# Rotary embedding from even-column and odd-column tiles of four heads, in place of a second up product with swapped columns

## The reference, cut to what matters

```python
q = (c_q @ w_up_q.T).reshape(b, s, 16, 64).transpose(0, 2, 1, 3)     # k likewise, from c_kv
e, o = (x[..., 0::2], x[..., 1::2])                                  # _apply_rope, q and k
rot = jnp.stack([e * cos - o * sin, e * sin + o * cos], axis=-1).reshape(x.shape)
scores = jnp.einsum('bhqd,bhkd->bhqk', q, k) * scale                 # softmax over these
out = jnp.einsum('bhqk,bhkd->bhqd', attn, v)
```

## Time and profile before

| | us |
|---|---|
| median of 3 runs | 1811.61 (1811.47 to 1812.64) |
| the profiled execution | 1810.62 |
| its span | 1808.7 |
| TensorE busy | 1649.7 (91%) |
| VectorE busy | 1577.7 (87%) |
| ScalarE busy | 1309.1 (72%) |
| GpSimd busy | 1306.5 (72%) |

### The profile page before, as it was taken

The page is one execution under the profiler, slowest core; times in us unless marked ns, Lnnn a source line. Parts: engine busy times, 40 slices in busy tenths (PEclk is TensorE's granted clock), DMA queues, the critical chain, the costliest instruction groups (busy, mean ns, idle before and its releaser), DMA issues. The chain is left out here.

```text
span 1808.7 us, 50674 instructions
## 1 busy us (share of the span) xinstructions
PE 1649.7 (91%) x20016; PEld 1027.2 (57%) x20016; DVE 1577.7 (87%) x3235; ACT 1309.1 (72%) x1876; POOL 1306.5 (72%) x926
## 2 busy tenths in 40 slices
PE   3888756999999999999999999999999999968888
PEld 2444431666666666666666666666666666644555
DVE  6999886999999998999999998999999998848885
ACT  4555462888888888888888888888888888855554
POOL 2343523888888888888888888888888888643444
PEclk9999976999999999999999999999999999988999
DMA  5000003111111112211111112211111112000000
GB/s 170 1 2 1 1 1 70 37 37 37 37 37 37 37 41 52 53 37 37 37 37 37 37 40 54 52 37 37 37 37 37 37 39 52 20 1 1 13 13 25
DMA packets 46665, 63.49 MB, mean 35 GB/s; under 512 B 9312, under 2 KB 21600, under 8 KB 46176
## 3 DMA queue, kind: packets, MB, share of 16 engines
q1 hardware_dynamic: 43632, 59.41, 13.7%
q10 hardware_dynamic: 2800, 0.85, 0.2%
HBM read 7.67 MB, written 2.10 MB: 5 GB/s over the span
## 5 line engine op out<-in xcount | busy, mean ns | idle before, releaser
L1222 POOL TENSOR_TENSOR area<-area 128x1024 f16<-128x1024 f32 (+1 forms) x512 | 833.1, 1645 | 159.9 <-ACT area L1190 137.7
L1116 DVE TENSOR_REDUCE area<-ps 128x1 f32<-128x512 f32 x1024 | 668.8, 685 | 60.5 <-PE ps L996 52.4
L1188 ACT ACTIVATE area<-ps 128x1024 f16<-128x1024 f32 x512 | 524.6, 1025 | 233.8 <-PE ps L1023 233.0
L1042 PE MATMUL ps<-cv_all,area 128*128 128x64 f16 x4096 | 458.6, 195 | 0.0
L1040 PE MATMUL ps<-cv_all,area 128*128 128x65 f16 x4096 | 456.8, 193 | 1.5 <-POOL area L1222 1.5
L1044 PE MATMUL ps<-cv_all,area 128*128 128x65 f16 x4096 | 455.3, 192 | 0.0
L1042 PEld LDWEIGHTS ps<-cv_all,area 128*128 128x128 f16 x4096 | 381.3, 97 | 86.1
L1040 PEld LDWEIGHTS ps<-cv_all,area 128*128 128x128 f16 x4096 | 384.0, 97 | 51.6 <-POOL area L1222 1.4
L1022 PE MATMUL ps<-area 128*128 128x512 f16 x1024 | 390.0, 381 | 18.6 <-DVE area L1140 17.7
L996 PE MATMUL ps<-area 128*128 128x512 f16 x1024 | 394.8, 386 | 8.6 <-DMA area<-area 5.7
L1023 PE MATMUL ps<-area 128*128 128x512 f16 x1024 | 388.7, 380 | 0.0
(11 more groups left out here) (175 smaller groups left out, 2727.9 us busy)
## 6 DMA issues: line engine op xcount, KB each, us to landing
area<-area SPq DMA_DIRECT2D x384, 128.0 KB, 2.4
xg<-in_x SPq DMA_DIRECT2D x4, 512.0 KB, 7.5
area<-in_wup SPq DMA_DIRECT2D x1, 2048.0 KB, 10.5
out_x<-xg SPq DMA_DIRECT2D x3, 512.0 KB, 3.2
cs<-in_rope SPq DMA_DIRECT2D x1, 1024.0 KB, 11.5
area<-area SPq DMA_DIRECT2D x64, 2.0 KB
area<-in_wo ACTq DMA_DIRECT2D x1, 512.0 KB, 7.5
area<-in_wg SPq DMA_DIRECT2D x1, 512.0 KB, 8.4
```

What stands on the lines that cost most here:

```text
L1042: nc.tensor.matmul(o[:, 0:DH], p_hi[:, s % 4, c:c + P], latents[:, DH + 1:CV], start=False, stop=False, skip_group_check=True)
L1116: nc.vector.tensor_reduce(mx[:, hd, kh, qt:qt + 1], bank, AX.X, ALU.max).then_inc(s_mr, 1)
L1188: nc.scalar.activation(p_hi[:, s % 4, :], sc, ACT.Exp, scale=0.125).then_inc(s_e16, 1)
L1222: nc.gpsimd.tensor_tensor(p_lo[:, s % 4, c0:], src[:, (s // 2) % 2, :], p_hi[:, s % 4, c0:], ALU.subtract).then_inc(s_pp, 1)
```

## The change

Weight columns are split in even and odd ones (`up_columns`), 128 of each hold 32 pairs of four heads, and a chunk now serves four heads, which is two units (a group). An R item is the up product of the even or of the odd columns; each is multiplied by cosine and by sine (2 VectorE instructions an item), and GpSimd makes `even*cos - odd*sin` and `odd*cos + even*sin` (2 instructions a chunk). ScalarE casts both in one instruction of 1024 columns; GpSimd makes the low halves in two. A unit now runs 2 chunks: 4 R items in steps 6, 7, 14 and 15. A head's 64 rows now lie in `qk` as 32 even and 32 odd ones, which come from two tiles: `stack` copies 32 partitions at a time, 24 copies a unit. The buffers grow (`area` from 26 to 30 K words, r_hi and r_lo to three buffers of two halves). The plan of items is new, and so is the prologue: 14 R items (7 chunks), and the first scores are issued 6 items before its end. The transposition of the maxima uses the plain identity, and the factor 1/64 moves to the VectorE instruction behind it.

```diff
-            "aa aaa aT Tmrb rb Prbb rbb Pbbb bb rbbb rbb rccn rc ccc cc cc".split())}
+            "aa aaaa Tm Tbb Pb Pbbb rb rbb bb bbbb bcn ccc c ccc rc rc".split())}
...
-        before = [letters[c].pop(0) for c in "rrrrrrrrssssaaaaaassaaaaaassaaaambbbbbbbbbb"]
+        before = [letters[c].pop(0) for c in "rrrrrrrrrraaaaaarraaaaaarraaaambbbbbbbbbb"]
...
+        SUMS, CASTS, LOWS = {1: (6, 0), 3: (6, 1), 9: (7, 0), 11: (7, 1)}, {4: 6, 12: 7}, {5: (6, 0), 7: (6, 1), 13: (7, 0), 15: (7, 1)}
...
                     elif kind == "A":
                         if i == 0 and hd == 0:
-                            pe.wait_ge(s_sq, (w + 1) * 96)
-                            pe.wait_ge(s_sk, (w + 1) * 96)
+                            pe.wait_ge(s_sq[slot], (w // 2 + 1) * 192)
+                            pe.wait_ge(s_sk[slot], (w // 2 + 1) * 192)
...
-                        nc.vector.tensor_tensor((ra, rb)[sw][:, c % 2, :], bank, cs[:, sw, 512 * half_:512 * half_ + 512],
-                                                ALU.mult).then_inc(s_mr, 1)
+                        nc.vector.tensor_tensor(ra[:, c % 2, i, :], bank, cos, ALU.mult)
+                        nc.vector.tensor_tensor(rb[:, c % 2, 1 - i, :], bank, sin, ALU.mult).then_inc(s_mr, 1)
...
-                    nc.gpsimd.tensor_tensor(rc[:, c % 2, :], ra[:, c % 2, :], rb[:, c % 2, :], ALU.add).then_inc(s_rc, 1)
+                    nc.gpsimd.tensor_tensor(rc[:, c % 2, i, :], ra[:, c % 2, i, :], rb[:, c % 2, i, :],
+                                            (ALU.subtract, ALU.add)[i]).then_inc(s_rc, 1)
...
-                    nc.scalar.copy(r_hi[:, c, :], rc[:, c % 2, :]).then_inc(s_rh, 1)
+                    nc.scalar.copy(r_hi[:, b_, h_], rc[:, c % 2]).then_inc(s_rh, 1)
...
                 def stack(w, slot):
-                    for kind, done in ((0, s_sq), (2, s_sk)):
-                        for sm in (s_rh, s_rl):
-                            sp.wait_ge(sm, w * 4 + (kind + 2))
+                    for kind, done in ((0, s_sq), (1, s_sk)):
+                        sp.wait_ge(s_rh, 4 * group + 2 * kind + 2)
+                        sp.wait_ge(s_rl, 2 * (4 * group + 2 * kind + 2))
                         for hd in range(2):
-                            rows = slice(64 * hd, 64 * hd + 64)
-                            hi, lo = (t[rows, kind:kind + 2, :].rearrange("p c n -> p (c n)") for t in (r_hi, r_lo))
+                            head = 2 * (w % 2) + hd
+                            for i in range(2):
+                                hi, lo = (t[32 * head:32 * head + 32, b_, :, i, :] for t in (r_hi, r_lo))
...
-                                sp.dma_start(qk[name_][row:row + 64, slot, hd, :], src).then_inc(done, 16)
+                                    row += 32 * i
+                                    sp.dma_start(qk[name_][row:row + 32, slot, hd, :].rearrange("p (h n) -> p h n", h=2),
+                                                 src).then_inc(done[slot], 16)
```

More of the change, by code:

```diff
@@ L33 @@
 UNITS = B * PAIRS
+GROUPS = UNITS // 2
+HALF = H * DH // 2
 EPS = 1e-5
@@ L46, in rope_tables @@
     sin = np.concatenate([np.sin(freqs), np.sin(freqs)], -1)[:, ::2]
[L47 to L50, removed]
+    return np.stack([np.tile(cos.T[:DH // 2], (4, 1)), np.tile(sin.T[:DH // 2], (4, 1))], 1).astype(np.float32)
 def up_columns(wq, wk):
-    swap = np.arange(H * DH) ^ 1
-    four = np.stack([w[:, i] for w in (np.transpose(wq), np.transpose(wk)) for i in (np.arange(H * DH), swap)], 1)
+    four = np.stack([np.transpose(w)[:, i::2] for w in (wq, wk) for i in range(2)], 1)
     return np.concatenate([four, four], 0)
@@ L353, in build @@
         s_rc, s_rh, s_rl = sem("rotated_sum"), sem("rotated_hi"), sem("rotated_lo")
-        s_sq, s_sk = sem("q_stacked"), sem("k_stacked")
+        s_sq, s_sk = ([sem(f"{n}_stacked_{k}") for k in range(2)] for n in "qk")
         s_mm, s_mmz, s_mrow = sem("max_columns_done"), sem("max_columns_zeroed"), sem("max_row_stored")
@@ L625, in turn @@
                                                     ALU.subtract).then_inc(s_hl, 1)
-                            if first and last and 3 <= k < 11:
-                                up_low(pool, k - 3)
+                            if first and last and k in (3, 5, 7, 9):
+                                up_low(pool, k // 2 - 1)
                     if first:
@@ L956, in items, with buffer_of, rotation_read @@
         def items(s, left):
-            return [i for i in plan[s] if i[1] <= left]
+            u = UNITS - 1 - left
+            return [i for i in plan[s] if (2 * u + i[1] < CHUNKS if i[0] == "R" else i[1] <= left)]
         def read_by(item, left):
             return [i for s in range(STEPS) for i in items(s, left)].index(item) + 1
+        def buffer_of(c):
+            return ((c // 4) % 2, 2)[(c // 2) % 2], c % 2
+        def rotation_read(c):
+            if c < 7:
+                return read_before[("R", c, 0, 1)]
+            u = (c - 7) // 2
+            n = len(before) + sum(len(items(s, UNITS - 1 - v)) for v in range(u) for s in range(STEPS))
+            return n + read_by(("R", c - 2 * u, 0, 1), UNITS - 1 - u)
         def run_units(prologue, unit):
@@ L984, in misc @@
                     if kind == "R":
[L985 to L988, removed]
+                        c = 2 * u + off
+                        kind_, half_ = (c // 2) % 2, c % 2
+                        which = 2 * kind_ + i
+                        j0, t0 = P * ((c // 4) % 4), S * (c // 16) + 512 * half_
+                        src = (cq_t, ckv_t)[kind_][:, t0:t0 + 512]
                         nc.tensor.matmul(bank, wup[:, which, 0, j0:j0 + P], src, start=True, stop=False)
@@ L999, in misc @@
                         pe.wait_ge(s_mm, w * 2 + (hd + 1))
-                        last = nc.tensor.matmul(bank[:, 0:P], mm[:, hd, :], ident_64th[:], start=True, stop=True)
+                        last = nc.tensor.transpose(bank[:, 0:P], mm[:, hd, :], ident[:])
                     elif kind == "OT":
@@ L1050, in prologue @@
                         misc(item, 0, 0, n, n % 2)
-                    for s in range(2):
-                        scores(0, 0, s, 0)
-                        scores(0, 0, s, 1).then_inc(s_s, 1)
+                        if n == len(before) - 6:
+                            for s in range(2):
+                                scores(0, 0, s, 0)
+                                scores(0, 0, s, 1).then_inc(s_s, 1)
                 def unit(u, k, left, n, par):
@@ L1108, in misc @@
                     if kind == "R":
-                        c, half_, sw = i // 2, (i // 2) % 2, i % 2
-                        if not (w == 0 and c < 2):
-                            v.wait_ge(s_rc, w * 4 + (c - 1))
-                        nc.vector.tensor_tensor((ra, rb)[sw][:, c % 2, :], bank, cs[:, sw, 512 * half_:512 * half_ + 512],
-                                                ALU.mult).then_inc(s_mr, 1)
+                        c = 2 * u + off
+                        cos, sin = (cs[:, t, 512 * (c % 2):512 * (c % 2) + 512] for t in range(2))
+                        if c >= 2:
+                            v.wait_ge(s_rc, 2 * (c - 1))
+                        nc.vector.tensor_tensor(ra[:, c % 2, i, :], bank, cos, ALU.mult)
+                        nc.vector.tensor_tensor(rb[:, c % 2, 1 - i, :], bank, sin, ALU.mult).then_inc(s_mr, 1)
                     elif kind == "A":
@@ L1194, in exps, with rot_hi @@
                         nc.scalar.activation(ps[:, 2, :], ps[:, 2, :], ACT.Exp, scale=0.125).then_inc(s_ea, 1)
[L1196 to L1199, removed]
-                    nc.scalar.copy(r_hi[:, c, :], rc[:, c % 2, :]).then_inc(s_rh, 1)
+                def rot_hi(c):
+                    act.wait_ge(s_rc, 2 * (c + 1))
+                    group, kind = c // 4, (c // 2) % 2
+                    if kind == 0 and group >= 2:
+                        for slot in range(2):
+                            act.wait_ge(s_sq[slot], (group - 1) * 192)
+                    if kind == 1 and group >= 1:
+                        for slot in range(2):
+                            act.wait_ge(s_sk[slot], group * 192)
+                    b_, h_ = buffer_of(c)
+                    nc.scalar.copy(r_hi[:, b_, h_], rc[:, c % 2]).then_inc(s_rh, 1)
                 def prologue():
-                    for w in range(2):
-                        for c in range(4):
-                            rot_hi(w, c)
+                    for c in range(6):
+                        rot_hi(c)
                     exps(0, 0)
@@ L1211, in unit @@
                             exps(u * STEPS + (s + 1), (s + 1) % STEPS)
-                        if left >= 2 and s in ROT_HI:
-                            rot_hi(u + 2, ROT_HI.index(s))
+                        if s in CASTS and 2 * u + CASTS[s] < CHUNKS:
+                            rot_hi(2 * u + CASTS[s])
                 run_units(prologue, unit)
@@ L1245, in unit @@
                         low(u * STEPS + s, s)
```

(3 more changed lines are left out.)

86 lines of the change are left out of this document (46 added, 40 removed).

## The result

1924.7 us median (1919.2 to 1929.5, 4 runs) against 1811.5 us: ratio 1.062, 95% interval [1.060, 1.065]. Forecast was 1880; slower, as the likeliest case said, and at the upper end of the range. The profiled execution took 1920.8 us, 110.1 more than that of before.

The account below looks back on a forecast made before the run. PE was taken as the bound, DVE close behind. 29 units at 2.1 us give 61; with 3.8, -1.7, +7 and -1 that makes 69 on the profiled 1810.6: 1880 us, the forecast's own range 1835 to 1925, of all 1780 to 1925.

Parts of the forecast that it names:

- R items: PE in each unit: 4 in place of 8 take off 1.72 us.
- the likeliest case: Whole kernel: the forecast itself, slower at 1880 us, chance 0.56.
- T0: The moment a unit's last score matmul is done and its first copy is issued.
- the second rival: Loop: issue is cheap but DVE takes half the gain, unit 39.9 us, time 1790 us, chance 0.10.
- The price of an issue: SP queue in stack: each of 24 copies costs 0.637 us, unchanged by halving its bytes.
- both rivals with a cheap issue: SP queue: smaller copies issue faster; 1763 us (chance 0.17), or 1790 us with DVE as the bound (0.10).
- T0 to the b item: Next unit's first b item waits for all 24 copies, landed at T0 + 18.1; PE waits 3.0 us.
- The rest of the unit: From the b item to the next T0: 24.9 us falls to 23.9.
- The clock: PE at half clock behind the wait for copies costs 0.8 us a unit, bounds 0 and 2.8.
- the fourth rival: Loop: half clock behind every wait, the full 2.8 us a unit, time 1940 us, chance 0.13.
- Unit 30: No R items on either side, so wait and clock stand bare: 3.8 us more.
- Prologue and unit 0: Prologue +7 us to the first exponentials, fewer low halves in ffn("f1") -1, unit 0 -1.7.

Follow-up runs that it names:

- e1: The changed kernel with its 24 copies a unit ordered by head and a semaphore for each head: 1784.7 us, ratio 0.985.
- e3: The changed kernel with 12 copies of 64 partitions from the even tiles alone, odd columns left out of the scores: 1777.1 us, ratio 0.981.
- e2: The kernel before with each copy cut into two of 32 partitions, 24 a unit, nothing else changed: 1919.3 us, ratio 1.059.
- e4: The changed kernel with 14 unread matmuls of 512 columns ahead of the first b item's wait for the copies: 1887.6 us, ratio 1.042.

## Why the prediction was right in kind and 45 us short

*R items.* Right, less than counted: PE was at the first b item at T0 + 14.55 rather than 15.1, but of 1.72 us a unit only 1.3 is left in e1 and e3 (39.44 against 40.72). PE's busy time did fall by 1.72 (40.08 to 38.36), but its idle time rose from 0.64 to 1.07, and the waits in it are for VectorE: the second rival's mechanism at a smaller price. The prediction also passed over where the R items end: in the changed kernel unit 28 has two and unit 29 none, before they ended with unit 29. In e1 unit 29 takes 36.4 us, so of its 27 us some 4 are from this unit; in the changed kernel the wait hides it (42.9).

*The price of an issue.* The term that decided, and right: 597 ns. "Bytes don't set it" holds in e2 and e3 too. So both rivals with a cheap issue fall. The rule of the Trainium skill named beside it ("DMA: Bandwidth & Descriptors", section "Rules for kernel authors": coalesce) agrees: e2 is that rule broken alone, 108 us.

*T0 to the b item.* Forecast 18.1 us; measured 18.11 in the mean of 30 (17.4 to 19.3). That it fits to the tenth is luck: the last issue started at 15.9 in the mean rather than 15.65, and landed 2.1 behind that rather than 2.4. PE's wait was 3.5 rather than 3.0, since it arrived 0.5 earlier.

*The rest of the unit.* Mis-sized: 23.9 forecast, 24.5 measured in e4 and in the five stretches of the changed kernel without half clock. The step that failed is "loses what the first part doesn't of the 1.72": 24.9 fell only to 24.5 (in e1 not at all: a typical unit has 24.88, and PE's waits for VectorE in it rose from 2.4 us to 3.4). 0.6 x 29 = 17 us. The changed kernel's five units without half clock took 42.0 to 42.4, near the 42.0 of the forecast, but by luck: in them the b item came at T0 + 17.5 to 17.9. With the mean of 18.1 it would be 42.6.

*The clock.* Mis-sized: 0.8 forecast, 1.36 measured. From the b item to the next T0 PE takes 24.51 us with no half clock (5 units), 26.1 with one stretch of 3.4 us (21), 27.3 with twice that (2). The one left, 24.79, is unit 29, without R items (22.96 at full clock in e4). e4 gives 1.4 by another way. "PE is full on both sides of this wait" didn't protect it. 0.56 x 29 = 16 us. The rule of the Trainium skill cited for the fourth rival ("TensorE: Matmul & The Clock Gate", section "HAM oscillation — how this bites in real kernels") agrees in kind, in 24 of 29 units; its rival's price, the full 2.8 us a unit, was seen in two.

*Unit 30.* 3.8 forecast, 6.5 measured, at a granted clock of 0.92 over the unit; with the wait filled (e4) the unit took 40.55, 3.2 more than before.

*Prologue and unit 0.* +7 - 1 - 1.7 forecast, +10.5 - 0.2 measured, 6 us more. The first A item, SyncE's queue and VectorE in the changed kernel:

```profile
300.30 1.01 PE L1007 MATMUL ps<-area 128*128 128x512 f16 x2 [14.15 <-DMA area<-area]
```

```profile
282.76 31.37 SPq L1294 DMA_DIRECT2D area<-area  x48
318.94 0.77 SPq L1299 DMA_DIRECT2D area<-area  x1
```

```profile
317.83 0.17 DVE L1132 TENSOR_REDUCE max_columns<-area 128x8 f32<-128x16 f32 x1
318.63 0.28 DVE L1137 TENSOR_SCALAR area<-ps 8x128 f16<-8x128 f32 x1 [0.63 <-PE ps L1011]
```

The copies came as forecast: the first A item started at 300.30 (forecast 300.4). The row of maxima was issued the moment VectorE had read it, 5 us after the last copy of stack(1) was issued, so "behind stack(1)" was wrong here. Mis-sized is the stretch between: the reductions and multiplies took 17.5 us where 15 were counted, and the transposition and its reading 1.1 more. Of the 10.5, the count of copies costs 3.8: in e3, with half of them, the first A item starts at 296.46 and the exponentials at 319.72. The other 6.6 lie with the rest of the new prologue, which no run takes apart. Granted clock was 0.50 from 276.6 to 324.4 in the changed kernel; before, it was 0.50 from 283.1 to 300.2 and from 303.6 to 313.9, and 1.00 around these. Whether that is cause or result of the slower prologue no run here tells.

The terms: 17 + 16 + 3 + 6 = 42 of the 41 us between 69 and 110; the last 4 are the distance of the profiled execution, 1920.8, from the median.

## What to carry to other kernels

Count the DMAs, not their bytes, when a layout change cuts copies in two, and set the row of issues against the work that lies between the first issue and the first reader. If it no longer fits, ask first whether the first reader needs all of them: ordering by reader and a semaphore for each turned +6.2% into -1.5% without one copy less. Then look at who else the longer row blocks (the buffers that it reads, what else is in the queue): freeing these, with VectorE's order, was the next 1%.

## What the runs showed that was not expected

A wait of about 3.5 us in an otherwise full PE, once in 44 us, brought a stretch of 3.4 us or more at half clock in 24 of 29 units. In e2, where the wait was 2.2 us in the mean, it came in 16 of 29; with the wait filled, in none. The length of the wait alone doesn't decide: in two units in a row the b item started at T0 + 17.48, and a stretch at half clock followed in the first and not in the second.

A copy within SBUF took 591 to 612 ns to issue for 64 KB and 128 KB, in one or two pieces a partition; it landed 2.0 to 2.1 us after the start of its issue for 64 KB and 2.4 us for 128 KB.

Left open: whether the copies spread over a second queue would do as well as their order, which wasn't tried, and what makes the new prologue 6.6 us longer apart from the copies.
